# A two-layer recurrence: loop turns of two engines moved, and three small moves on VectorE

## The reference

```python
def step(carry, xw_t):            # layer 0, xW = x @ Wx + b for all steps
    prev_h, prev_c = carry
    a = xw_t + prev_h @ Wh
    i, f, o = sigmoid(a[:, :H]), sigmoid(a[:, H:2*H]), sigmoid(a[:, 2*H:3*H])
    g = tanh(a[:, 3*H:])
    next_c = f * prev_c + i * g
    next_h = o * tanh(next_c)
...
def step(h, xt):                  # layer 1
    m = concatenate([xt, h]) @ weight + bias
    g, c = sigmoid(m[:, :units] + 1.0), tanh(m[:, units:])
    h_new = g * h + (1.0 - g) * c
...
x = x + layer0(x)
x = x + layer1(x)
```

## Time and profile before

| | us |
|---|---|
| three runs | 232.51, 232.40, 231.21 |
| median | 232.4 |
| the profiled execution | 231.32 |
| its span, first to last instruction | 229.7 |
| around the span | 1.6 |

### The profile page before, as it was taken

The page is one execution under the profiler, slowest core; times in us unless marked ns, Lnnn a source line. Parts: engine busy times, 40 slices in busy tenths (PEclk is TensorE's granted clock), DMA queues, the critical chain, the costliest instruction groups (busy, mean ns, idle before and its releaser), DMA issues.

```text
span 229.7 us, 12849 instructions
## 1 busy us (share of the span) xinstructions
PE 223.8 (97%) x4850; PEld 207.4 (90%) x4850; DVE 201.5 (88%) x1557; ACT 121.5 (53%) x778; POOL 4.4 (2%) x12
## 2 busy tenths in 40 slices
PE   7999999999999999999999999999999999999994
PEld 5799999999999998999999999999999999999882
DVE  6788989988889898899888998998989989899894
ACT  3645555555555555555555555555555555555551
POOL 1500000000000000000000000000000000000000
PEclk9999999999999999999999999999999999999997
DMA  6000001010010001000010000100001000000000
GB/s 191 18 16 27 14 27 49 14 30 24 15 45 23 11 23 44 23 14 23 23 35 23 23 11 23 46 11 23 23 18 40 23 22 13 27 14 14 16 16 11
DMA packets 11970, 6.22 MB, mean 27 GB/s; under 512 B 1446, under 2 KB 11692, under 8 KB 11948
## 3 DMA queue, kind: packets, MB, share of 16 engines
q1 hardware_dynamic: 11792, 5.66, 8.7%
q10 hardware_dynamic: 156, 0.27, 0.3%
HBM read 3.82 MB, written 2.10 MB: 26 GB/s over the span
## 4 chain that ended last, share of the span: by engine, by line
PE 72%; DVE 19%; ACT 3%; DMA 1%; issue 1%; SPq 1%
PE a L284 14%; PE gate_f L258 11%; PE a L242 7%; PE a L276 6%; PE gate_o L226 4%; PE gate_i L226 4%; PE gate_g L226 4%; DVE cell_bank L572 3%; PE gate_f L226 3%; PE gate_g L264 3%; PE gate_o L264 3%; PE gate_i L264 3%; ACT act_bank L487 3%; PE gate_i L268 2%; PE a L278 2%; DVE hT L579 2%
## 5 line engine op out<-in xcount | busy, mean ns | idle before, releaser
L258 PE MATMUL gate_f<-hT,wh_raw 128*128 128x32 f32 x254 | 49.0, 275 | 0.2
L258 PEld LDWEIGHTS gate_f<-hT,wh_raw 128*128 128x128 f32 x254 | 37.8, 188 | 11.6 <-DVE hT L579 8.2
L472 ACT ACTIVATE forget<-gate_f 128x32 f32<-128x32 f32 x127 | 25.0, 197 | 36.9 <-PE gate_f L258 36.7
L492 ACT ACTIVATE acts<-a 128x64 f32<-128x64 f32 x128 | 28.6, 223 | 28.1 <-PE a L284 28.1
L579 DVE TENSOR_TENSOR hT<-out_gate,act_bank 128x32 f32<-128x32 f32 x128 | 24.1, 188 | 21.6 <-ACT act_bank L487 21.6
L487 ACT ACTIVATE act_bank<-cell_bank 128x32 f32<-128x32 f32 x128 | 23.3, 182 | 35.5 <-DVE cell_bank L572 35.5
L276 PE MATMUL a<-h_high,w1x_part 128*128 128x32 f16 x768 | 41.8, 176 | 0.3 <-ACT w1x_part L464 0.2
L284 PE MATMUL a<-acts,w1h_part 128*128 128x32 bf16 x762 | 39.3, 178 | 0.0
L572 DVE TENSOR_TENSOR_SCAN cell_bank<-scan_mul,scan_add 128x64 f32<-128x64 f32 x128 | 38.7, 302 | 0.4 <-ACT scan_add L472 0.3
L278 PE MATMUL a<-h_low,w1x_fp 128*128 128x32 f16 x256 | 35.4, 176 | 0.0
L284 PEld LDWEIGHTS a<-u_rest,w1h_part 128*128 128x128 bf16 x508 | 31.4, 98 | 1.5
(11 more groups left out here) (96 smaller groups left out, 631.7 us busy)
## 6 DMA issues: line engine op xcount, KB each, us to landing
xT<-in_x_dram SPq DMA_DIRECT2D x46, 64.0 KB, 1.8
out_dram<-outT SPq DMA_DIRECT2D x32, 64.0 KB, 1.6
wx_s<-in_L_cond_Wx_dram SPq DMA_DIRECT2D x1, 256.0 KB, 2.8
wh_raw<-in_L_cond_Wh_dram ACTq DMA_DIRECT2D x1, 256.0 KB, 3.1
w_raw<-in_L_cond_weight_dram SPq DMA_DIRECT2D x1, 256.0 KB, 3.6
bias_rows<-in_biases_dram ACTq DMA_DIRECT2D x1, 3.0 KB
condT<-in_cond_dram SPq DMA_DIRECT2D x1, 16.0 KB, 2.9
```

Of the source, the lines that this page charges most:

```text
L258: nc.tensor.matmul(gate_step(GATE_F, j), wh_raw[:, GATE_F * P:(GATE_F + 1) * P], hT[:, (j - 1) % RING, :], start=False, stop=True, skip_gr ...
L472: return nc.scalar.activation(out, gate_step(q, j), func)
L492: nc.scalar.activation(acts1[:, 0:3:2, i, :], a1_step(j).rearrange("p (g n) -> p g n", g=2), ACT.Tanh).then_inc(acts1_ready, 1)
```

## The change

Four edits. (1) TensorE: the block that adds Wh h to the four gates of step s (h_ready, `forget_sum`, `high`, `low`) becomes a function `gates`, and of each body's first step it is issued at the end of the body before, so the loop turns between the gates and `layer1_input`. (2) VectorE: `layer1_low` of a body's last step moves to the head of the next body, so the loop turns between `scan` and `u_low`. (3) `add_layer1` (outT) moves to the place of `add_layer0` (x1T), ahead of h_low, and x1T to the place of outT, between `pair` and u. (4) The waits for x and for the result's buffer stand behind the scan of the step ahead of their use, with a count that is the same for all.

```diff
+            def gates(s, j, first):
+                pe.wait_ge(h_ready, s)
+                forget_sum(j)
...
+                high(GATE_O, j)
+                low(GATE_O, j, o_summed)
...
                 for j in range(BODY):
                     s, m, k = s0 + j, j // GS, j % GS
                     r, l = s - 1, (j - 1) % BODY
+                    if j > 0:
+                        gates(s, j, first)
                     if not (first and j == 0):
-                        pe.wait_ge(h_ready, s)
-                        forget_sum(j)
...
                     if ends and k not in (0, 2, 4):
                         warm(0, 4 if k in (5, 7) else 2)
+                if not last:
+                    gates(s0 + BODY, 0, False)
...
-            def add_layer0(s, j, x_count):
+            def add_layer0(s, j):
...
                 dve.wait_ge(h_ready, s + 1)
-                if j % HS == 0:
-                    dve.wait_ge(x_in[slot], x_count)
...
-            def add_layer1(j, free):
+            def add_layer1(j):
...
-                if j % HS == 0:
-                    dve.wait_ge(out_free[slot], free)
...
             def body(s0, first):
+
+                if not first:
+                    layer1_low(s0 - 3, BODY - 3)
                 for j in range(BODY):
...
                         hidden(s - 1, l0)
-                        add_layer0(s - 1, l0, s0 + 16 if j else s0)
+                    if not (first and j < 3):
+                        add_layer1(l2)
+                    if not (first and j == 0):
                         hidden_low(s - 1, l0)
...
                         layer1_pair(s - 2, l1)
-                    if not (first and j < 3):
-                        add_layer1(l2, s0 + 16 if j > 2 else s0)
+                    if not (first and j == 0):
+                        add_layer0(s - 1, l0)
...
                     scan(s)
-                    if layer1_runs:
+                    if layer1_runs and j < BODY - 1:
                         layer1_low(s - 2, l1)
...
+                    if j % HS == 0:
+                        dve.wait_ge(x_in[j // HS], s0 + 16)
+                    if j % HS == 2:
+                        dve.wait_ge(out_free[j // HS], s0 + 16)
```

More of the change, by code:

```diff
@@ L339, in _ @@
             project1(0, 0, 0, 0)
+            def gates(s, j, first):
+                pe.wait_ge(h_ready, s)
+                forget_sum(j)
+                if first and j == 1:
+                    pe.wait_ge(wh_split, 4)
+                pe.wait_ge(high_ready, s)
+                high(GATE_I, j)
+                if first and j == 1:
+                    pe.wait_ge(fp16_ready, 1)
+                pe.wait_ge(low_ready, s)
+                low(GATE_I, j, i_summed)
+                high(GATE_G, j)
+                low(GATE_G, j, g_summed)
+                high(GATE_O, j)
+                low(GATE_O, j, o_summed)
             def body(s0, first, last):
@@ L613, in layer1_low @@
                                         ALU.subtract).then_inc(u_low_ready, 1)
-            def add_layer0(s, j, x_count):
-                i, slot = j % RING, j // HS
+            def add_layer0(s, j):
+                i = j % RING
                 dve.wait_ge(h_ready, s + 1)
-                if j % HS == 0:
-                    dve.wait_ge(x_in[slot], x_count)
                 nc.vector.tensor_tensor(x1T[:, i, :], hT[:, i, :], xT[:, j * N:(j + 1) * N],
                                         ALU.add).then_inc(x1_ready, 1)
-            def add_layer1(j, free):
+            def add_layer1(j):
                 i, slot, o = j % RING, j // HS % SLOTS, j % HS * N
-                if j % HS == 0:
-                    dve.wait_ge(out_free[slot], free)
                 nc.vector.scalar_tensor_tensor(out=outT[:, slot, o:o + N], in0=u_of(j), scalar=0.5,
@@ L664, in _ @@
             body(T - BODY, False)
+            layer1_low(T - 3, BODY - 3)
             hidden(T - 1, BODY - 1)
-            add_layer0(T - 1, BODY - 1, T)
+            add_layer1(BODY - 3)
             hidden_low(T - 1, BODY - 1)
             layer1_pair(T - 2, BODY - 2)
-            add_layer1(BODY - 3, T)
+            add_layer0(T - 1, BODY - 1)
             layer1_state(T - 2, BODY - 2)
@@ L672, in _ @@
             layer1_low(T - 2, BODY - 2)
-            add_layer1(BODY - 2, T)
+            add_layer1(BODY - 2)
             layer1_pair(T - 1, BODY - 1)
@@ L676, in _ @@
             dve.wait_ge(u_ready, T + 1)
-            add_layer1(BODY - 1, T)
+            add_layer1(BODY - 1)
 _INS = ["x", "cond_1024", "L0_cond_Wx", "L0_cond_Wh", "biases", "L1_cond_weight"]
```

## The result

| | us |
|---|---|
| before, median of 6 runs | 232.37 |
| the changed kernel, median of 6 runs | 234.50 |
| ratio, 95% interval | 1.0101 (1.0071 to 1.0131) |
| profiled execution before / after | 231.32 / 234.48 |
| its span | 229.7 / 232.9 |

The changed kernel is slower by 2.1 us, 1.0%, and the interval lies clear of 1. The forecast was 233.6 (+1.2), the range 231.4 to 235.4.

What follows compares the result with a forecast made beforehand. It took the chain from hT through gate_f, forget, keep and scan as the bound, 1.69 us a step. Five turns +1.35, loop entry -0.05 and edit 3 -0.1 made +1.2: 233.6 on the median, range 231.4 to 235.4.

Steps and rivals of the forecast that it cites:

- rival 2: TensorE's turn makes layer 1 so late that VectorE's queue holds up the scan: +2.9, 235.3 us; chance 0.14.
- The plain step: hT to hT away from the loop's turns: stays 1.69 us, set by the chain through keep.
- Edit 2, u_low and hT late: VectorE at the turn: u_low starts 0.56 us behind the scan, hT 0.66, making hT 0.11 late.
- Edit 1, gate_f's load behind u_low: TensorE at the turn: gate_f's load waits behind late u_low, 0.39 us behind hT, 0.15 late.
- Layer 1 behind TensorE's turn: `layer1_input`'s first load some 0.8 us behind gate_f's, keep 0.19 late; bounds 0 and 0.52.
- The turn: Each of five times the loop goes back: lateness 0.45 us in sum instead of 0.18.
- -0.48: Moved waits take x's count off the way to h_low: 0.08 us saved six times.
- Rival 1: The turns are hidden because u_low comes in time: all 1.0 us goes, 231.4; chance 0.13.
- Rival 3: h_low decides the plain step, 0.01 us shorter over 112 steps: -1.1 beside the turns' +1.2, 232.5; chance 0.08.

Runs made afterwards that it cites:

- edit 1 alone: The kernel before with only TensorE's gates block issued ahead of the loop's turn; ratio 1.0028 (1.0001 to 1.0056).
- edit 2 alone: The kernel before with only VectorE's turn moved between scan and u_low; ratio 1.0087 (1.0052 to 1.0122).
- edit 4 alone: The kernel before with only the waits for x and the result's buffer moved behind the scan of the step ahead; ratio 1.0045 (1.0018 to 1.0072).
- edit 4 undone: The changed kernel with the waits for x and the result's buffer back at their users; ratio to the kernel before 1.0034 (1.0009 to 1.0060).
- Edit 3 alone: The kernel before with only outT ahead of h_low and x1T behind the second pair, waits with them; ratio 0.9998 (0.9970 to 1.0025).
- the written-out steps: The kernel before with steps 16 to 111 written out for TensorE, ScalarE and VectorE, without a loop; ratio 0.9956 (0.9930 to 0.9982).

## Why the prediction was right, and where not

**Sign and range** held: +2.1 against +1.2, inside 231.4 to 235.4. "Within 1%" had 0.81 and "slower by over 1%" 0.15; the ratio lies on that edge. That the time is in the range is in part luck. The turns cost 0.6 less than the sum had, the straight-line bodies, which it had at nothing, cost 1.3, and the two misses partly offset each other. The range's upper part was there for rival 2, which did not happen.

**The plain step** stayed 1.69, as said, and edit 3 doesn't touch the chain.

**Edit 2, u_low and hT late.** Predicted u_low 0.56 behind the scan, hT 0.66, an interval 0.11 too long. Measured 0.50, 0.61 and 0.06. From VectorE's branch (117.4) to u_low it is 0.4 with the new register step in it, where 0.40 and 0.08 more were taken.

**Edit 1, gate_f's load behind u_low.** Predicted 0.39 behind hT and 0.15 too long, measured 0.40 and 0.17. The mechanism (u_low takes the place of the branch) is borne out by edit 1 alone, where u_low is in time and the second interval falls to 1.68, and by edit 2 alone, where u_low and the branch add up and it rises to 2.04. What the step left out: pair is late too (0.65 behind hT), because u_low's lateness also delays layer 1's activations. Keep, four places behind pair in the queue, starts at 118.97, 0.04 behind forget's end at 118.93: two chains are late by nearly the same amount there, and no run takes them apart.

**Layer 1 behind TensorE's turn.** Predicted `layer1_input` 0.80 behind gate_f and keep late by 0.19, measured 0.69 and 0.11 (1.03 behind hT against 0.92). The branch is 0.3 behind gate_f's load (118.6, 118.28) where 0.38 was worked out, and the load 0.37 behind the branch instead of 0.42: the sequencer runs a little further ahead of the loads than assumed. Rival 2 asked for 0.40 and falls.

**The turn** thus costs 0.35 instead of the 0.45 in the sum, and the loop with its entry +0.7 instead of +1.3 (the five turns +0.8, a stall of 0.07 in the first pass less).

**Edit 4 is the step that failed.** The prediction put -0.48 on it, with its register step hidden "between the scan and hT", and booked nothing against it; of the -0.48 its sum kept the 0.08 at the loop's entry and saw the rest given back to layer 1. In place of it the runs show two things. First, +1.3 in the 32 straight-line steps: where counts are constants there is no register step to carry the wait; it lands on hT, tanh's wait becomes an instruction of its own in front, and each such hT is 0.07 late, 13 times behind step 4 (5 in steps 4 to 15, 8 from step 111 on), and one of them by 0.38 more, the cause of which is open (edit 4 alone has all of it, with edit 4 undone all of it is gone). "Behind the waits is hT" was written down, and the conclusion was not drawn. Second, nothing of the -0.48 shows in the changed kernel. Edit 3 alone brings the third interval's 0.08 (1.69) as edit 4 alone does; in the changed kernel that interval is set by layer 1 (1.80 with edit 4 and without it). The 0.08 at the entry doesn't go with x's count either: the interval there is 1.77 before and after and 1.76 with edit 4 alone, and pair stands late in it (0.55 behind hT before, 0.56 after).

**Rival 1**, hidden turns, falls: 0.50 between scan and u_low. The Trainium skill's 108 ns for a compare-and-branch ("Advanced Engine Details and Errata", section Control Flow Timing) stands against 0.3 to 0.4 us from a taken branch to the next instruction on VectorE and TensorE in every turn of 16 steps shown here, and over 3 us where the body has 32 steps. Rival 3 falls by edit 3 alone.

**A better version** than both: edit 3 alone takes 0.5 off the loop, and the written-out steps take 1.1 off; the second is the only one that a ratio tells from before (0.9956, interval 0.9930 to 0.9982; with edit 3 0.9953, 0.9921 to 0.9986).

## What to carry to other kernels

A wait that is met long ago is free only if its carrier is: look in the order of instructions at which instruction a moved wait lands on, in the loop and outside of it, and keep it off the one that the critical chain waits for. A loop's turn costs 0.3 to 0.4 us from the branch to the next instruction on its engine in these loops of 16 steps, and what stands behind it is late by that, so put behind it what nobody waits for within that time, and check the instruction's consumers on the other engines, not only its own queue. With two edits that aim at the same 0.08 us, count it once.

## What the runs showed of the hardware that was not expected

- Two waits on one VectorE instruction: 21 ns for the separate wait, but the instruction starts 0.07 us later where the wait that is split off is the last to be met (hT, edit 4 alone), with a second wait as old as x's first piece too. On u_low the second wait costs nothing: it starts 0.20 behind the scan with it and 0.21 without.
- From a branch back over 457 VectorE records or 2470 of TensorE to the engine's next instruction it is 3.0 and 4.0 us, over 230 and 1236 it is 0.3 to 0.4; ScalarE's next record stands 0.3 behind a branch over 226. TensorE's granted clock falls to 0.50 behind that stall, and a turn costs 4.9 us in all.
- 96 steps of code that runs once are no slower than a loop over 16, apart from 0.004 a step in one of the two kernels.
- Single intervals of 0.3 to 0.45 over the rest that move when VectorE's code moves, even inside a loop whose instructions stay the same. Their cause is open.
- TensorE's fp32 loads take 0.33 instead of 0.19 us up to where the record of the granted clock begins, at 5.0 us in one execution and 9.9 in another, and 0.33 again where the granted clock is 0.50. Between those two executions it is worth some 1.1 us.
